# A layer-norm, recurrence and ternary-weight block on eight cores: the last weight chunk in two transfers, one sum matmul, paced fillers, statistics by pairs, and another order of work up to the third pair

## The reference

```python
xn = _layernorm(x, axis=-1)
x = x + _L0_attn_ref(xn, ...) + _L0_ffn_ref(xn, ...)
# _L0_attn_ref: S = 64 states, D = 2048
a = jnp.tanh(xn @ Wa.T + ba); b = jnp.tanh(xn @ Wb.T + bb)
h[t] = a[t] * h[t-1] + b[t]                  # scan over the 4096 rows
return xn + h @ Wout.T + bout
# _L0_ffn_ref: a 2048 x 2048 weight
scale = jnp.mean(jnp.abs(weight))
w_t = jnp.clip(jnp.round(weight / (scale + 1e-10)), -1.0, 1.0)
return xn @ (w_t * scale).T + bias
```

## Time and profile before

| what | value |
| --- | --- |
| device time, three runs | median 569.41 us, lowest 568.62 us |
| the profiled execution | 568.35 us |
| its spans, first to last instruction | 562.4 us (core 1) to 566.0 us (core 4) |
| the page's busy shares | PE 87%, DVE 61%, ACT 46%, POOL 29% |
| the page's DMA mean | 151 GB/s |

### The profile page before, as it was taken

The page is one execution under the profiler, slowest core; times in us unless marked ns, Lnnn a source line. Parts: engine busy times, 40 slices in busy tenths (PEclk is TensorE's granted clock), DMA queues, the critical chain, the costliest instruction groups (busy, mean ns, idle before and its releaser), DMA issues.

```text
span 565.3 us, 9294 instructions; the slowest of 8 cores (562.4 to 566.0 us)
## 1 busy us (share of the span) xinstructions
PE 494.4 (87%) x2742; PEld 250.0 (44%) x2742; DVE 343.2 (61%) x513; ACT 262.3 (46%) x233; POOL 162.8 (29%) x590
## 2 busy tenths in 40 slices
PE   0020799997789999999999999999999999999996
PEld 0010344543434555555555545454545454545542
DVE  3533597782766575758484848474756675663542
ACT  0476594526362635353626363635445353627100
POOL 1500464363234050605050414132232324140000
PEclk9999999997899999999999999999999999999999
DMA  7999941441513829282828274737474655531324
GB/s 235 340 337 333 288 161 65 146 163 19 216 45 103 197 76 224 75 221 75 201 73 190 100 166 133 161 119 154 129 155 143 139 161 121 179 112 38 101 49 112
DMA packets 16997, 85.58 MB, mean 151 GB/s; under 512 B 2162, under 2 KB 2162, under 8 KB 10802
## 3 DMA queue, kind: packets, MB, share of 16 engines
q1 hardware_dynamic: 16272, 83.89, 52.3%
q0 software_dynamic: 384, 1.05, 1.2%
q10 hardware_dynamic: 292, 0.05, 0.1%
HBM read 52.48 MB, written 33.55 MB: 152 GB/s over the span
## 4 chain that ended last, share of the span: by engine, by line
PE 77%; DMA 7%; SPq 4%; DVE 4%; issue 3%; POOLq 3%; ACT 1%; DVEq 1%; POOL 0%; ACTq 0%
PE pu L647 58%; DMA wbuf<-wt 7%; PE pu L619 6%; PE ptr L595 5%; PE pab L606 4%; SPq L250 4%; DVE bst L391 1%; PE pu L660 1%; PE pu L665 1%; PE pu L673 1%; PE pu L655 1%; DVE xnT L447 1%; POOLq L776 1%; DVEq L393 1%; ACT xnT L310 1%
## 5 line engine op out<-in xcount | busy, mean ns | idle before, releaser
L407 DVE SCALAR_TENSOR_TENSOR sx<-pu,scl,sx 128x512 f32<-128x512 f32 x212 | 158.1, 750 | 170.1 <-PE pu L647 60.3
L647 PE MATMUL pu<-wbuf 128*128 128x512 f16 x896 | 206.8, 379 | 0.0
L647 PE MATMUL pu<-wbuf,xnT 128*128 128x512 f16 x672 | 157.6, 381 | 0.0
L647 PEld LDWEIGHTS pu<-wbuf 128*128 128x128 f16 x896 | 86.5, 98 | 97.0
L310 ACT COPY xnT<-ptr 128x1024 f16<-128x1024 f16 x64 | 64.5, 1008 | 91.2 <-PE ptr L595 91.2
L647 PEld LDWEIGHTS pu<-wbuf,xnT 128*128 128x128 f16 x672 | 64.9, 98 | 74.2 <-issue 1.6
L391 DVE BATCH_NORM_STATS2 bst<-sx 128x6 f32<-128x512 f32 x128 | 78.8, 677 | 8.0 <-DMA sx<-x 8.0
L595 PE MATMUL ptr<-sidn,xnT 128*128 128x128 f16 x512 | 41.5, 227 | 42.1 <-ACT xnT L298 25.1
L298 ACT ACTIVATE xnT<-sx,nmr,yr 128x2048 f16<-128x2048 f32 x32 | 66.8, 2088 | 23.6 <-POOLq L789 23.6
L768 POOL TENSOR_SCALAR uu<-mv 128x1 f32<-128x1 f32 x32 | 8.6, 269 | 225.2 <-DVE mv L395 195.8
L305 ACT ACTIVATE sx<-sx,nmr,p1r 128x2048 f32<-128x2048 f32 x32 | 67.0, 2096 | 0.0
(11 more groups left out here) (61 smaller groups left out, 314.4 us busy)
## 6 DMA issues: line engine op xcount, KB each, us to landing
sx<-x SPq DMA_DIRECT2D x32, 1024.0 KB, 8.9
y<-sx SPq DMA_DIRECT2D x63, 512.0 KB, 4.0
wbuf<-wt SPq DMA_DIRECT2D x16, 1024.0 KB, 31.2
wab_s<-wab POOLq DMA_DIRECT2D x1, 512.0 KB, 11.4
y<-sx SPq DMA_DIRECT2D x2, 256.0 KB, 3.9
wocv<-wo POOLq DMA_DIRECT2D x1, 256.0 KB, 14.4
wbuf<-wo POOLq DMA_DIRECT2D x2, 128.0 KB, 3.9
sidn<-idn ACTq DMA_DIRECT2D x1, 32.0 KB, 8.0
```

The source lines that it names most:

```text
L407: vector.scalar_tensor_tensor(out, bank(b), scl[:, :], out, OP.mult, OP.add).then_inc(s_ev, 1)
L647: ins = tensor.matmul(bank(b), left(p, lname, c), right(rname, c, h), start=(fresh and c == 0), stop=(state is None and c == HC - 1), skip ...
```

## The change

It does seven things. (1) The last weight chunk is loaded as two transfers of 1024 columns, with a semaphore each; ACT and DVE each sum 512 columns of the first half when it has landed, and 512 of the second. (2) All partial sums are in one tile `acc` with 19 columns, and one matmul adds them. (3) The fillers are 5 after chunk 14, 4 after the first half of chunk 15, 2 after the second half, and 6 behind the sum. (4) Chunk 0 is rounded and clipped in two halves of 1024 columns; TensorE begins with the four units that need only the first half. (5) A chain works on both tiles of a pair at once (128 x 2), and waits for the statistics of both; there are 16 chains instead of 32. (6) DVE takes the statistics of tiles 4 and 5 before `t1`, those of 7 and 6 before `t2`; `t2` is spread between evictions; `plain(15)` is evicted after `s4(2)`, directly ahead of `scan(2)`. (7) On TensorE the four `turn` of tiles 4 and 5 stand one unit earlier, and `gate(2)` ahead of `plain(15)`.

```diff
-N_AA = len(ABS_ACT) + 1
-N_AD = len(ABS_DVE) + 1
+N_AA = len(ABS_ACT) + 2
+N_AD = len(ABS_DVE) + 2
...
-            for c in range(NCH):
+            for c in range(NCH - 1):
                 sync.dma_start(out=wslot(c), ...
+            c = NCH - 1
+            sync.dma_start(out=wbuf[:, c * D:c * D + HD],
+                           in_=wt_d[128 * c:128 * (c + 1), 0:HD]).then_inc(s_w[c], 16)
+            sync.dma_start(out=wbuf[:, c * D + HD:(c + 1) * D],
+                           in_=wt_d[128 * c:128 * (c + 1), HD:D]).then_inc(s_wl, 16)
...
             def norm(t):
-                scalar.wait_ge(s_stats, POS[t] + 1)
+                scalar.wait_ge(s_stats, t // 2 + 1)
...
-            absum(NCH - 1, N_AA - 1, 0, D // 2)
+            absum(NCH - 1, N_AA - 2, 0, QW)
+            absum(NCH - 1, N_AA - 1, HD, HD + QW)
...
-            rounded(0)
+            for lo in (0, HD):
+                vector.tensor_scalar(wint[:, lo:lo + HD], wslot(0)[:, lo:lo + HD],
+                                     inv[:, :], None, OP.mult).then_inc(s_rnv, 1)
+            for i, lo in enumerate((0, HD)):
+
+                vector.wait_ge(s_rnv, 2)
+                vector.tensor_scalar(wpart(0, lo, lo + HD), wint[:, lo:lo + HD],
+                                     -1.0, 1.0, OP.max, OP.min).then_inc(s_tern, 1)
...
             for u in range(6):
                 plain(u)
-
+            stats(4)
+            stats(5)
             for c in range(0, HC, 2):
                 t1(c)
...
             tensor.wait_ge(s_w[NCH - 2], 16)
-            busy(8)
+            busy(5)
+            tensor.wait_ge(s_w[NCH - 1], 16)
+            busy(4)
+            tensor.wait_ge(s_wl, 16)
+            busy(2)
             tensor.wait_ge(s_aa, N_AA)
-            tensor.matmul(pab[:, 256:256 + N_AA], ones[:, :], acc_a[:, :],
-                          start=True, stop=True)
             tensor.wait_ge(s_ad, N_AD)
-            tensor.matmul(pab[:, 256 + N_AA:256 + N_AA + N_AD], ones[:, :],
-                          acc_d[:, :], start=True, stop=True).then_inc(s_sum, 1)
-            busy(10)
+            tensor.matmul(pab[:, 256:256 + N_AA + N_AD], ones[:, :], acc[:, :],
+                          start=True, stop=True).then_inc(s_sum, 1)
+            busy(6)
...
-            def chain(t):
-                i = t % 4
-                m = mv[:, 2 * i:2 * i + 1]
-                r = yr[:, i:i + 1]
-                g.wait_ge(s_mv, POS[t] + 1)
-                if t >= 4:
-                    g.wait_ge(s_xnb, POS[t - 4] + 1)
-                    g.wait_ge(s_v, POS[t - 4] + 1)
+            def chain(n):
+
+                i = 2 * (n % 2)
+                both = mv[:, 2 * i:2 * i + 4].rearrange("p (t s) -> p s t", s=2)
+                r = yr[:, i:i + 2]
+                g.wait_ge(s_mv, 2 * n + 2)
+                if n >= 2:
+                    g.wait_ge(s_xnb, 2 * (n - 2) + 2)
+                    g.wait_ge(s_v, 2 * (n - 2) + 2)
```

More of the change, by code:

```diff
@@ L338, in absum @@
                 scalar.wait_ge(s_w[c], 16)
+                if hi > HD and lo > 0:
+                    scalar.wait_ge(s_wl, 16)
                 if i >= 1:
@@ L427, in absum @@
                 vector.wait_ge(s_w[c], 16)
-                vector.tensor_reduce(acc_d[:, i:i + 1],
+                if hi > HD and lo > QW:
+                    vector.wait_ge(s_wl, 16)
+                vector.tensor_reduce(acc[:, N_AA + i:N_AA + i + 1],
                                      wbuf[:, c * D + lo:c * D + hi], axis=AX.X,
@@ L493, in _ @@
                 absum(c, i, 0, D)
-            absum(NCH - 1, N_AD - 1, D // 2, D)
+            absum(NCH - 1, N_AD - 2, QW, HD)
+            absum(NCH - 1, N_AD - 1, HD + QW, D)
             vector.wait_ge(s_sum, 1)
@@ L529, in _ @@
             plain(9)
-            stats(5)
             t3(4)
@@ L534, in _ @@
             plain(11)
+            stats(ORD[6])
+            stats(ORD[7])
             vector.wait_ge(s_T, 8)
-            for c in range(0, HC, 2):
-                t2(c)
+            t2(0)
             plain(12)
+            t2(2)
             plain(13)
-            stats(ORD[6])
+            t2(4)
+            t2(6)
             plain(14)
-            plain(15)
             s13(2)
@@ L545, in _ @@
             s4(2)
+            plain(15)
             scan(2)
-            stats(ORD[7])
             for p in range(2, NP):
@@ L727, in _ @@
             plain(10)
+            turn(4, 0)
             plain(11)
-            turn(4, 0)
+            turn(4, 1)
             plain(12)
-            turn(4, 1)
+            turn(5, 0)
             plain(13)
-            turn(5, 0)
+            turn(5, 1)
             plain(14)
-            turn(5, 1)
+            gate(2)
             plain(15)
-            gate(2)
             for p in range(2, NP):
@@ L757, in _ @@
             g.memset(two_i[:, :], 2)
[L759 to L766 removed]
+            def chain(n):
[6 more added lines that the diff above has]
+                    g.wait_ge(s_v, 2 * (n - 2) + 2)
                 g.drain()
[L768 to L769 removed]
+                g.tensor_scalar(uu[:, :], both[:, 1, :], EPS_LN, None, OP.add)
                 g.drain()
@@ L784, in chain @@
                 g.drain()
-                g.tensor_tensor(nmr[:, i:i + 1], m, r, OP.mult)
-                g.tensor_scalar(p1r[:, i:i + 1], r, 1.0, None, OP.add)
+                g.tensor_tensor(nmr[:, i:i + 2], both[:, 0, :], r, OP.mult)
+                g.tensor_scalar(p1r[:, i:i + 2], r, 1.0, None, OP.add)
                 g.drain()
-                g.tensor_scalar(nmr[:, i:i + 1], nmr[:, i:i + 1], -1.0, None, OP.mult)
+                g.tensor_scalar(nmr[:, i:i + 2], nmr[:, i:i + 2], -1.0, None, OP.mult)
                 g.drain().then_inc(s_stats, 1)
             chain(0)
-            chain(1)
             g.wait_ge(s_w[NCH - 3], 16)
@@ L801, in _ @@
             g.drain().then_inc(s_hrow, 1)
-            for t in ORD[2:6]:
-                chain(t)
+            chain(1)
+            chain(2)
             g.wait_ge(s_unit, 14)
@@ L808, in _ @@
             g.dma_start(out=wo2[64:128, :], in_=wo_d[:, HD:D]).then_inc(s_wo2, 16)
-            for t in ORD[6:]:
-                chain(t)
+            for n in range(3, NP):
+                chain(n)
     return nc
```

43 lines of the change are left out of this document (24 added, 19 removed).

## The result

The changed kernel takes 561.18 us (median of four, 560.68 to 562.65) against 568.62 for the kernel before beside it: the ratio is 0.987, 95% interval 0.984 to 0.990. A second set of runs gave 0.9875 (0.9855 to 0.9895). So it is 1.3% faster, more than the measurement's uncertainty and less than 2%. The forecast was 557.0 with a range to 561.5: the time lies 4.2 us above the forecast, at the range's upper edge. The profiled run took 560.68 us. Runs in which a die was disturbed are left out of all medians and ratios here; with the one of 587.31 us the median of the kernel before was 569.01.

A forecast was written before the change was run, and what follows sets the result against it. TensorE was taken to bound the kernel, with the threshold and a hole at 128 to 165 us to win: 566.0 - 5.14 - 9.42 + 2.3 - 0.3 + 0.5 = 553.9, plus 0.4, 2.35 and 0.3: 557.0 us, range 555.3 to 561.5.

The forecast's parts named there:

- The total bytes are the same, so the last half lands when the chunk did.: Threshold, last weight chunk: splitting its transfer was taken to leave the landing of the last byte unchanged.
- Half sums, one matmul, fillers: Threshold: half sums gain 0.4 us, one sum matmul less gains 0.43, fillers ahead of the sum cost 0.3.
- Halves of chunk 0: Rounding of chunk 0 on DVE: two instructions more, 0.1 us each, cost 0.2 us.
- Tile 2: wait of 0.5 us: Tile 2's `turn`: a new TensorE wait for the chain of tiles 2 and 3, 0.5 us, bounds 0 and 1.6.
- Tiles 4 and 5: Chain ends at 113.0, norm(4) at 115.3, wanted at 116.4: no wait, 1 us in hand; the whole 5.14 us go.
- Tile 7: 2.3 us, both limits meeting: Tile 7's `turn`: wait of 1.8 us by ACT, 2.2 by POOL; 2.3 taken, bounds 1.8 and 4.3.
- The clock: Behind tile 7's wait: 2.3 us judged nearer to core 0's 1.95, where transposes stayed at the upper level.
- The slowest core: +0.4: Whole span: the slowest of eight cores draws the worst of clock and threshold, +0.4 us.
- `wo2` slowed by `t2`: Rival at pair 2: `wo2` load issues wait for `t2`, tile 7's wait is 4.3, clock falls: +3.7 us, 560.7; chance 0.2.
- Threshold gives nothing: Rival: threshold sum +0.3 instead of -0.3, tile 2 waits 1.6 instead of 0.5: +1.7 us, 558.7; chance 0.13.
- Two-wide chain dearer: Rival in regular pairs: 128 x 2 chain instructions cost more and TensorE waits in each of 13 pairs, slower; chance 0.03.
- Faster than forecast: Better case: wait 1.8 us at tile 7, none at tile 2, threshold -0.65: 555.3, the range's low side.

The follow-up runs named there:

- b: The kernel before with part 1 alone (chunk 15 in two transfers, sums of 512 columns): 570.18 us, ratio 1.0027.
- c: The changed kernel with GpSimd's loads of `wab` and `wocv` waiting for the last half of chunk 15: 562.51 us, ratio 0.9893.
- a: The changed kernel with part 1 undone: chunk 15 as one transfer, fillers 9 ahead of its landing and 2 behind: 559.97 us, ratio 0.9854.
- i: The changed kernel with chunk 15 in one transfer, `wo2` loads behind pair 3's chain and norm(7) ahead of states(2): 554.61 us, ratio 0.9753.
- e: The kernel before with parts 5 to 7 alone, nothing of parts 1 to 4: 559.54 us, ratio 0.9835.
- k: The kernel before with parts 5 to 7, `wo2` loads behind pair 3's chain and norm(7) ahead of states(2): 557.06 us, ratio 0.9786.
- f: The changed kernel with the two `wo2` loads behind the chain of pair 3: 558.89 us, ratio 0.9819.
- g: The changed kernel with the `wo2` loads behind pair 3's chain and norm(7) ahead of states(2) on ScalarE: 558.48 us, ratio 0.9816.
- after_again: The changed kernel once more, unaltered, as the control: 561.27 us, ratio 0.9875.
- d: The changed kernel with SP waiting for the first half of chunk 15 before it loads tiles 2 and 3: 561.26 us, ratio 0.9878.

## Why the prediction was off, point by point

Two steps failed: the last byte did not land when the chunk had, and the clock fell where nothing was counted for it. Going by the deciding core, the forecast's 553.9 became 558.0, 4.1 us more. It splits by rows: tile 2's turn was forecast at 94.28 - 0.3 + 0.5 = 94.5 and came at 96.45, +2.0; tile 4's wait, +0.45; pair 2 was forecast at 29.46 + 2.3 and took 33.46, +1.7; behind it 0.05 less. Around it, 0.4 that I had added for the slowest core falls away, and 2.68 outside the span instead of 2.35 and a median 0.5 above the profiled run instead of 0.3 make the 4.2 us between the two times. That the time is still within the range is luck: it lies outside the 554.5 to 559 of the forecast itself, and the range went to 561.5 for a rival that did not come true. Core 4's near hit is in part luck as well, since its last byte came only 0.25 us later than before and its clock stayed up.

**"The total bytes are the same, so the last half lands when the chunk did."** This step failed, and it is the largest term: in the means the last byte came 1.43 us later, and tile 2's turn 1.2 us later, where the sum had 0.2 (-0.3 + 0.5). In the six kernels with the split the last byte was seen at 62.8 to 64.2 (means, latest core up to 67.9); in the seven with one transfer, before among them, at 62.2 to 63.3 (latest 64.4). The gap to the chunk ahead is 4.1 to 5.4 against 3.4 to 3.9. b shows that it comes from part 1 alone. Shown by the packets' times: the 4 KB packets make the last megabyte 0.7 to 1.2 us longer, 0.8 on the mean of the seven profiled runs, which is more than half of the 1.3 us between the two groups. Not shown: what the rest is, the second completion or the GpSimd loads beside the longer transfer (c), since no run split the chunk with rows of full length. The Trainium skill (DMA: Bandwidth & Descriptors, 🔬 Queues, rings and completion order) says that a completion is counted only when all earlier writes of that DMA engine have landed; that fits with two completions behind a full queue, and no run isolates it.

**Half sums, one matmul, fillers.** From landing to `inv` the saving was 0.69 us; the terms gave -0.43 - 0.4 + 0.3 = -0.53. The half sums are 0.53 of it (b, 2.20 against 2.73; 0.69 us for 512 columns against 1.22), where I took 0.4. The one matmul and the other fillers give 0.25 (a, 2.48) to 0.33 (i, 2.40), where I took 0.43, and the 0.3 us for the fillers did not come, since TensorE had run dry before the landing. Halves of chunk 0 cost VectorE about the 0.2 that I took: 1.53 and 0.76 us for the four instructions, against 1.38 and 0.67 for a whole chunk's two on the same core. The stage from `inv` to tile 2's turn grew by more, 28.7 to 28.8 in the kernels that have the halves and the split (c apart), but only 28.3 to 28.4 in a and i (halves, no split) and 28.29 in b (split, no halves). The traces place it: VectorE's clip of chunk 1, the first instruction behind the two halves, starts 2.83 or 2.84 us behind `inv` on every core of the kernels with both, 2.55 to 2.57 with the halves alone and 2.42 without them; the next instructions add the rest. The profile shows nothing that it waits for (0.17 us of "issue" on core 6), and the cause stays open. What parts 2 to 4 are worth is not settled either: a and e, with and without them, differ by nothing that shows (559.97 and 559.54, from two sets), i and k by 2.4 us, of which the rows give them 0.27. The low bound of this sum was also wrong: its terms give -0.54, or -0.84 without the fillers' 0.3, and not -0.65; in the better case of the rivals the slowest core's 0.4 is left out.

**Tile 2: wait of 0.5 us.** There was none, on any core. On core 6 norm(2) runs from 93.97 to 96.06 and the turn follows at 96.45 without an idle TensorE; at the 2.34 us from norm to turn it could have come at 96.31, so 0.14 us were left. The term was within its bounds, and too high by its full size. **Tiles 4 and 5:** tile 5's wait and the slow matmuls behind it are gone, as forecast; the 1 us in hand at tile 4 was not there, and the turn waited 0.45 us for the norm behind this chain, which stood beside `t1` and two `t3`:
```profile
116.38 0.22 POOL L819 TENSOR_SCALAR nmr<-nmr 128x2 f32<-128x2 f32 x1 [0.15 <-issue]
```
I took 113.0 for this last instruction. Of the 3.4 us more on core 6, 2.0 are the later threshold; the chain started at 105.42, 0.6 late beyond that, and took 11.0 us instead of 10.2, with VectorE's operations in its way (1.27 and 0.99 us for instructions of 0.19). The forecast's 1 us in hand was an interpolation between the earlier trace rows, and too fine.

**Tile 7: 2.3 us, both limits meeting.** Right in the wait: 2.17 on four cores, 2.33 on one, 2.50 on two, 2.84 on one, most of them in steps of 0.33, the length of one chain instruction with its drain. So GpSimd is the limit, ScalarE's lies 0.4 below it at 1.78 (f). Both limits were right in mechanism and size, and the way to take the wait away followed: f 1.4 us in the means of that stage, 0.6 of wait and 0.8 of clock, and g 1.2 more, which is 2.0 of wait less 0.7 that comes back as waits at pair 3's turn.

**The clock.** I judged that 2.3 us is nearer to core 0's 1.95, where it stayed up, than to the 3.46 where it fell, and counted nothing. I overlooked a nearer row of the kernel before: behind the 2.83 us at tile 7's turn the eight transposes took 1.01 us, and the next eight matmuls were slow on seven of eight cores, here on core 4:
```profile
150.81 3.04 PE L647 MATMUL pu<-wbuf,xnT 128*128 128x512 f16 x8
```
In the changed kernel four of eight cores fell (0, 5, 6 and 7), and the slowest three are among them. From tile 7's turn to pair 3's the four took 30.92 to 31.13 us and the others 29.46, so a fall costs 1.5 to 1.7 us, 1.7 on the deciding core and 0.8 in the mean of eight; with after_again, a, c, d and e it is 24 of 48 cores. The length of the wait does not part them: of the changed kernel's waits of 2.17 and of 2.50 us some fell and some did not, and seven cores of b waited 2.82 or 2.83 us at the same turn with the next eight matmuls still at 1.89. All seven fell behind their next wait instead, 4.26 us at tile 6's turn. It is the second failed step: in a kernel timed by its slowest core, a loss that strikes every second core is likely to strike one that is late already, and cannot be counted as nothing.

**The slowest core: +0.4.** What this term should have held are the two losses above. Core 4 had been slowest before because its last byte came latest (63.11 against 62.23 on the mean) and because it lost most to the waits: its stage from tile 4 to pair 3's turn took 65.87 against 64.60 on the mean. So a sum for core 4 overstates what the change takes from the others. The mean span fell by 8.7 us, core 4's by 11.8, the largest by 8.0.

**The rivals.** *`wo2` slowed by `t2`*, 560.7: near the measured time, for another reason. 31 of 32 cores show the chain 4.0 to 5.3 us after the issue (4.2 to 5.5 before), and the issues took their usual 0.63 and 0.54 us, although a `t2` ran beside them for about 0.6 us or more on every one of these cores; one core showed the wait of 4.62, by late landing. So the port lock that the Trainium skill describes (SBUF — State Buffer, 🔬 SBUF: two separate sides) is visible in the chain's own instructions, 1.27 and 0.99 us for 0.19, and not in the issues. *Threshold gives nothing*, 558.7: its tile 2 part did not come; its threshold part did, larger than its bound of +0.3, since I had bounded the landing by nothing. *Two-wide chain dearer:* refuted, 0.19 us and the period unchanged at 29.46. *Faster than forecast* needed the 1.8 us wait, which came only with f.

## What to carry to other kernels

Splitting the last transfer of a full queue is not free: price the landing of the last part by itself, and test it alone (here 1.5 us slower) before the finer work behind it is counted. For a kernel timed by the slowest of eight cores, make the sum for the mean and for the worst core, since the core that is slowest before loses most of what you remove. When two limits meet at a wait, take both away; the first alone gave 1.4 us, of which 0.8 are the clock, the second 1.2. And look for the nearest row at which a loss did strike before it is counted as nothing.

## What the runs showed of the hardware that was not expected

- Two transfers of half a chunk, 4 KB rows, against one with 8 KB rows at the end of a saturated stream: 5% less rate over 12 us, and the last byte 1.3 us later (mean of the runs with and without, c left out). A 4 KB packet took 0.24 to 0.27 us, an 8 KB packet 0.38, in the same queue.
- The clock fell behind waits of 2.16 to 2.85 us (and one of 4.62) at tile 7's turn on 24 of 48 cores, and stayed up behind 1.77 to 1.93 us on all eight of f.
- GpSimd's next instruction behind its own two DMA issues and a drain started only when the second transfer had landed, 0.24 or 0.25 us after it on 64 of 64 cores: 4.1 us after the first issue where the second took 3.27 us to land, 6.1 where it took 5.24.
